# Layer 2 of the edges: one addition ahead of one set of transposes, and a deeper pipeline

## The reference

```
h = x @ W
loops = arange(n); src = [src, loops]; dst = [dst, loops]
deg = number of edges (self loop among them) into each node
out = segment_sum(h[src] / sqrt(deg[src] * deg[dst]), dst) + b
x   = layernorm(x + relu(out))
```

## Time and profile before

| What | us |
|---|---|
| median of 3 runs without a profile | 5666.66 |
| lowest and highest of them | 5656.37, 5669.94 |
| span of the profiled execution | 6076.0 |
| `edges2` in the profiled execution, from its first gather to the start of its last normalising activation | 4285.5 to 4873.0 |

### The profile page before, as it was taken

The page is one execution under the profiler, slowest core; times in us unless marked ns, Lnnn a source line. Parts: engine busy times, 40 slices in busy tenths (PEclk is TensorE's granted clock), DMA queues, the critical chain, the costliest instruction groups (busy, mean ns, idle before and its releaser), DMA issues. The chain is left out here.

```text
span 6076.0 us, 89008 instructions
## 1 busy us (share of the span) xinstructions
PE 4790.3 (79%) x21595; PEld 2959.6 (49%) x21595; DVE 4134.9 (68%) x7958; ACT 3755.8 (62%) x9127; POOL 4234.7 (70%) x4897
## 2 busy tenths in 40 slices
PE   6999999999999879998999899999588844551000
PEld 4555555555555434444444477777466633331000
DVE  5666666666666447777777799999466644557665
ACT  4777777777777534444444488888355555656665
POOL 6777777777777567666776177777666566676776
PEclk9999999999999989999999899999666655655555
DMA  4444444444444425554555499999455477875333
GB/s 109 122 122 124 116 126 120 116 126 119 123 123 116 111 87 174 153 151 148 157 154 147 155 362 363 365 362 343 139 156 158 144 261 243 292 269 171 125 121 98
DMA packets 513957, 1058.78 MB, mean 174 GB/s; under 512 B 123386, under 2 KB 193062, under 8 KB 513732
## 3 DMA queue, kind: packets, MB, share of 16 engines
q1 hardware_dynamic: 408372, 905.58, 44.1%
q0 software_dynamic: 100352, 149.23, 10.7%
q10 hardware_dynamic: 5008, 1.60, 0.1%
HBM read 648.47 MB, written 413.07 MB: 175 GB/s over the span
## 5 line engine op out<-in xcount | busy, mean ns | idle before, releaser
L786 ACT ACTIVATE p_s<-p_ps,cols 128x512 f32<-128x512 f32 x588 | 405.1, 689 | 377.2 <-PE p_ps L728 174.1
L1114 POOL DMA_INDIRECT ring_rows<-t_rows,home_cols x384 | 444.4, 1157 | 232.2 <-issue 91.7
L648 POOL DMA_INDIRECT home<-edge_row_cols,scatter_cols x392 | 428.9, 1094 | 233.6 <-issue 151.4
L147 POOL DMA_INDIRECT u_rows<-t_rows,home_cols x392 | 428.9, 1094 | 220.9 <-issue 116.8
L853 DVE TENSOR_TENSOR p_r<-p_s,p_r 128x512 f32<-128x512 f32 x588 | 402.4, 686 | 257.1 <-ACT p_s L786 188.8
L147 POOL DMA_INDIRECT ring_rows<-t_rows,home_cols x400 | 382.3, 956 | 232.1 <-issue 108.0
L154 POOL DMA_INDIRECT out<-u_res,scatter_cols x392 | 415.1, 1059 | 170.1 <-issue 123.3
L1103 POOL DMA_INDIRECT home_cols<-home,src_cols x380 | 389.3, 1024 | 147.7 <-issue 90.5
L1203 ACT ACTIVATE q_s<-q_ps,cols 128x512 f32<-128x512 f32 x294 | 202.4, 688 | 458.0 <-issue 144.6
L641 POOL DMA_INDIRECT p_xd<-in_x,dst_cols x388 | 408.8, 1054 | 105.2 <-issue 99.0
L641 POOL DMA_INDIRECT p_xs<-in_x,src_cols x388 | 392.7, 1012 | 125.1 <-issue 89.0
(11 more groups left out here) (298 smaller groups left out, 14313.3 us busy)
## 6 DMA issues: line engine op xcount, KB each, us to landing
p_x<-in_x SPq DMA_DIRECT2D x98, 512.0 KB
t_rows<-p_o SPq DMA_DIRECT2D x98, 512.0 KB
hT<-p_r SPq DMA_DIRECT2D x98, 512.0 KB
q_hn<-hT SPq DMA_DIRECT2D x98, 512.0 KB
r_h<-hT SPq DMA_DIRECT2D x98, 512.0 KB
r_x<-t_rows SPq DMA_DIRECT2D x98, 512.0 KB
t_rows<-r_y SPq DMA_DIRECT2D x98, 512.0 KB
t_rows<-r_x SPq DMA_DIRECT2D x98, 512.0 KB
```

The costliest lines, as they stand in the source:

```text
L147: nc.gpsimd.indirect_dma_start(out=rows[:, j, :], out_offset=None, in_=table, in_offset=bass.IndirectOffsetOnAxis(ap=idx[:, j:j + 1], axis ...
L648: nc.gpsimd.indirect_dma_start(out=tab["home"], out_offset=bass.IndirectOffsetOnAxis(ap=s["scat"][:, k:k + 1], axis=0), in_=s["at"][:, k:k ...
L786: nc.scalar.activation(act_out[i][:, :], flat(bank_r), ACT.Silu, bias=col(LS0 + i)).then_inc(r_act[i], 1)
L1114: nc.gpsimd.indirect_dma_start(out=rows[:, e % 4, j, :], out_offset=None, in_=tab["t1"], in_offset=bass.IndirectOffsetOnAxis(ap=s["home"][ ...
```

## The change

- The addition of the own rows moves in front of the transposes: DVE adds `both = rows + own` (both in SBUF, as they were loaded), PE transposes `both` alone, and the scan's result `run` goes straight into the product. The second set of four transposes and its bank `t_ps_t` are gone.
- So that the own row is counted once for each target, `dis` (one over the root of the degree, by which `nodes23` scales the rows it stores) is set to zero for edges that are not the last of their target.
- The four bias matmuls over 9 rows become one over 36 rows and 512 columns; `b2x36` holds the bias parts on a block diagonal, and `sdeg` is loaded as 36 rows of 128 in place of 9 rows of 512.
- The steps are spread: scan two steps behind the addition, product three, sum four, root five, apply six, store nine. All buffers of the stage are four deep. The straight code at the start is 16 steps in place of 8.

```diff
 # setup, nodes01
-  b2x9=sb("b2_x9", [9, H], BF16)
+  b2x36=sb("b2_x36", [9 * G, G, H], BF16)
+  nc.gpsimd.memset(s["b2x36"][:, :, :], 0.0)
-  for k in range(3):
-      sp.dma_start(s["b2x9"][3 * k:3 * k + 3, :], s["b2x3"][:, 0, :])
+  for j in range(G):
+      for k in range(3):
+          sp.dma_start(s["b2x36"][9 * j + 3 * k:9 * j + 3 * k + 3, j, :], s["b2x3"][:, 0, :])
-  nc.vector.reciprocal(s["dis"][:, :], s["sdeg"][:, :])
+  then(nc.vector.reciprocal(s["dis"][:, :], s["sdeg"][:, :]))
+  nc.vector.scalar_tensor_tensor(s["dis"][:, :], s["scat"][:, :], float(SKIP), s["dis"][:, :], ALU.is_lt, ALU.mult)
 # edges2
-  RING, UNROLL, FIRST, LOOP_TO = 8, 8, 8, EB // 8 * 8
+  RING, UNROLL, FIRST, LOOP_TO = 8, 8, 16, EB // 8 * 8
+  TO_SCAN, TO_PRODUCT, TO_GROW, TO_SUM, TO_ROOT, TO_APPLY, TO_STORE = 2, 3, 3, 4, 5, 6, 9
 # POOL
-  after(pool, s_turned, t - RING + 1)
+  after(pool, added, t - RING + 1)
 # PE, step(t)
-  if t.live(EB):
-      transpose4(nc, bank_s[t.of(2)], rows[:, t.of(RING)], s["ident"]).then_inc(s_turned, 1)
-      transpose4(nc, bank_t[t.of(2)], own[:, t.of(8)], s["ident"]).then_inc(o_turned, 1)
-  e = t.back(1)
-      after(pe, summed, e.b - 1)
-      pe.wait_ge(added, e.b + 1)
-      for j in range(G):
-          nc.tensor.matmul(bank_o[e.of(2)][:, j, :], sdeg[:, e.of(8), tile(j)], s["b2x9"][:, :], start=True, stop=False)
-          i = nc.tensor.matmul(bank_o[e.of(2)][:, j, :], both[:, e.of(2), tile(j)], s["w2"][:, :], start=False, stop=True)
+  e = t.back(TO_PRODUCT)
+      pe.wait_ge(scanned, e.b + 1)
+      after(pe, summed, e.b - 3)
+      nc.tensor.matmul(flat(bank_o[e.of(4)]), sdeg[:, e.of(8), :], b2x36 (512 columns), start=True, stop=False)
+      for j in range(G):
+          i = nc.tensor.matmul(bank_o[e.of(4)][:, j, :], run[:, e.of(4), tile(j)], s["w2"][:, :], start=False, stop=j == G - 1)
+  if t.live(EB):
+      pe.wait_ge(added, t.b + 1)
+      after(pe, scanned, t.b - 3)
+      transpose4(nc, bank_s[t.of(4)], both[:, t.of(4)], s["ident"]).then_inc(turned, 1)
 # DVE, step(t): new first instruction, and the lags
+      dve.wait_ge(rows_in[t.of(RING)], landed(RING, t, G))
+      dve.wait_ge(own_in[t.of(8)], landed(8, t))
+      after(dve, turned, t.b - 3)
+      nc.vector.tensor_tensor(both[:, t.of(4)], rows[:, t.of(RING)], own[:, t.of(8)], ALU.add).then_inc(added, 1)
-      nc.vector.tensor_tensor(both[:, t.of(2), :], run[:, t.of(2), :], flat(bank_t[t.of(2)]), ALU.add).then_inc(added, 1)
...
```

More of the change, by code:

```diff
@@ L1697, in ps @@
         def ps(name):
-            return [ctx.enter_context(nc.psum_tensor(f"{name}{i}", [P, G, P], F32)) for i in range(2)]
+            return [ctx.enter_context(nc.psum_tensor(f"{name}{i}", [P, G, P], F32)) for i in range(4)]
         sem = phase_semaphores(nc, ctx, "edges2", sum(to_edges2.values(), []))
-        RING, UNROLL, FIRST, LOOP_TO = 8, 8, 8, EB // 8 * 8
-        rows, own, cont, sdeg = ring["rows"], ring["own"], ring["cont"], sb("t_sdeg", [9, 8, BLK], BF16)
-        run, both = sb("t_run", [P, 2, BLK]), sb("t_both", [P, 2, BLK])
-        degs = sb("t_degs", [P, 2, G])
+        RING, UNROLL, FIRST, LOOP_TO = 8, 8, 16, EB // 8 * 8
+        TO_SCAN, TO_PRODUCT, TO_GROW, TO_SUM, TO_ROOT, TO_APPLY, TO_STORE = 2, 3, 3, 4, 5, 6, 9
+        STEPS = EB + TO_APPLY
+        rows, own, cont, sdeg = ring["rows"], ring["own"], ring["cont"], sb("t_sdeg", [9 * G, 8, P], BF16)
+        both, run = sb("t_both", [P, 4, G, H]), sb("t_run", [P, 4, BLK])
+        degs = sb("t_degs", [P, 4, G])
         od, v, o = sb("t_od", [P, 4, G, H]), sb("t_v", [P, 4, G, H]), sb("t_o", [P, 4, G, H])
@@ L1721, in _ @@
         def _(sp):
-            for t in range(EB + 8):
+            for t in range(EB + TO_STORE):
                 if t < EB:
                     if t >= 7:
-                        after(sp, o_turned, t - 7)
+                        after(sp, added, t - 7)
                         after(sp, grown, t - 7)
@@ L1776, in step @@
                     nc.scalar.activation(sd[:, e.of(4), :], guard[:, e.of(4), :], ACT.Sqrt).then_inc(rooted, 1)
-                if t.live(EB):
-                    act.wait_ge(own_in[t.of(8)], landed(8, t))
-                    act.wait_ge(picked, t.b + 1)
-                    after(act, summed, t.b - 3)
+                e = t.back(TO_GROW)
+                if e.live(EB):
+                    act.wait_ge(own_in[e.of(8)], landed(8, e))
+                    act.wait_ge(picked, e.b + 1)
+                    after(act, summed, e.b - 3)
                     for j in range(G):
-                        i = nc.scalar.activation(od[:, t.of(4), j, :], own[:, t.of(8), j, :], ACT.Copy,
-                                                 scale=degs[:, t.of(2), j:j + 1])
+                        i = nc.scalar.activation(od[:, e.of(4), j, :], own[:, e.of(8), j, :], ACT.Copy,
+                                                 scale=degs[:, e.of(4), j:j + 1])
                     i.then_inc(grown, 1)
-                e = t.back(3)
+                e = t.back(TO_APPLY)
                 if e.live(EB):
@@ L1810, in step @@
                     nc.vector.reciprocal(rs[:, e.of(4), :], sd[:, e.of(4), :]).then_inc(inverted, 1)
-                if t.live(EB):
-                    dve.wait_ge(scanned, t.b + 1)
-                    dve.wait_ge(o_turned, t.b + 1)
-                    after(dve, product, t.b - 1)
-                    nc.vector.tensor_tensor(both[:, t.of(2), :], run[:, t.of(2), :], flat(bank_t[t.of(2)]),
-                                            ALU.add).then_inc(added, 1)
-                e = t.back(2)
+                e = t.back(TO_SCAN)
+                if e.live(EB):
+                    dve.wait_ge(turned, e.b + 1)
+                    dve.wait_ge(cont_in[e.of(8)], landed(8, e))
+                    after(dve, scanned, e.b)
+                    after(dve, product, e.b - 3)
+                    nc.vector.tensor_tensor_scan(run[:, e.of(4), :], cont[:, e.of(8), :], flat(bank_s[e.of(4)]),
+                                                 initial=run[:, e.back(1).of(4), BLK - 1:BLK] if e.past(1) else 0.0,
+                                                 op0=ALU.mult, op1=ALU.add).then_inc(scanned, 1)
+                e = t.back(TO_ROOT)
                 if e.live(EB):
```

58 lines of the change are left out of this document (26 added, 32 removed).

## The result

| | before | changed |
|---|---|---|
| median, us (9 runs each) | 5666.66 | 5679.51 |
| lowest and highest, us | 5656.37, 5670.89 | 5670.21, 5684.39 |
| ratio, with its 95% interval | | 1.0022 (1.0013 to 1.0032) |

The change makes the kernel 12.9 us slower. The forecast was 5596 us, 70 us faster, with a range of 5548 to 5636: wrong in sign.

A forecast was written before the change was run, and what follows sets the result against it. Prediction: a PE-DVE exchange bounds `edges2`; with POOL's pace instead, 461.3 + 18.8 + 10 + 5.6 + 16.8 us end it at 4798.0, a gain of 75.5, scaled to 70: 5596 us, range 5548 to 5636.

The forecast's parts named there:

- What bounds the kernel now: Step on `edges2` before: no engine is full; PE and DVE wait for each other in turn, making 587.5 us.
- the exchange at 5.96 us a block: In `edges2`, DVE's sum waits for PE's product and PE's product for DVE's addition, setting 5.96 us a block.
- the third rival: In `edges2`, unprofiled PE runs at the high clock, POOL already bounds, only the ends move: 5660 us; chance 0.08.
- The runs take 0.933 of the span; I scale.: Whole kernel: unprofiled runs take 0.933 of the profiled span, so the gain of 75.5 us was scaled to 70.
- Order, buffers and pace of the changed stage: Changed `edges2`: the ping-pong goes, POOL sets 5.03 us a block, DVE waits for gathered rows at no cost.
- The worked end of the stage: Changed `edges2`: summed from first gather at 4285.5, its last activation ends at 4798.0, against 4873.5 before.
- The collision: In `edges2`, gathers beginning during L1807, with two SBUF inputs, wait for its end: 18.8 us, bounds 0 and 52.
- The start: Start of `edges2`: PE's instructions arrive late in the straight code, partly covered: 10 us, bounds 0 and 25.
- the rival of the starved straight code: Start of `edges2`: further straight steps deliver PE's matmuls every 1.40 us, 20 us slower, 5686 us; chance 0.04.
- The end: End of `edges2`: 5.6 us for the last gather to land, then 16.8 us of DVE's last steps.
- The exchange isn't there without the profile: Rival on `edges2`: unprofiled, before is already bound by POOL and gains 0 to 15 us, 5660 us; chance 0.08.
- The change doesn't do what it says: Rival on `edges2`: the wait moves to landing gathers, POOL 5.6 us a block, 5635 us; chance counted within the forecast.

The follow-up runs named there:

- e4: The kernel before with one bias matmul of 36 rows and 512 columns in place of four of 9 rows: 6072.55 us, ratio 1.0010.
- e9: The changed kernel with rows and own added by PE in the bank, without the addition on DVE: 6030.04 us, ratio 1.0020.
- e7: The kernel before plus one unread DVE addition a block with both inputs in SBUF: 5683.16 us, ratio 1.0031.
- e8: The kernel before plus one unread DVE addition a block with one input in PSUM: 5671.63 us, ratio 1.0013.
- e15: The changed kernel with rows and own added by PE in the bank, without the addition on DVE, run again: 5668.70 us, ratio 1.0001.
- e16: The changed kernel as it is, run again on the chip of e15: 5678.44 us, ratio 1.0022 to the kernel before.
- e5: The changed kernel as it is, run again on a second chip: 5678.76 us, ratio 1.0021 to the kernel before.
- e6: The kernel before, unchanged, run again for its profile on the chip of e5: 5670.46 us, ratio 1.0007.
- e3: The changed kernel with each lag from the scan on one step shorter: 6137.97 us, ratio 1.0124 to the kernel before.

## Why the prediction was wrong, point by point

**"What bounds the kernel now", the exchange at 5.96 us a block: the step that failed.** The kind that was timed doesn't have the pace of the earlier trace rows. There POOL was the bound (3.7 us of waits in 430). With POOL already full, 75.5 us could not be there to gain. On kind A the change is worth 60 us when POOL has three gathers a block, and nothing before.

The exchange didn't set the 5.96 us on kind B either. The prediction read correctly that PE waits for the addition there. PE's waits from 4300 to 4860 us, in the profile that it read:

```profile
PE t_ps_o L1762 <- issue: 83.4, 45, 6.9
```

The label is "issue", but 29 of these pauses are over 1 us, and every one ends 0.05 to 0.15 us after an addition has ended. In the earlier trace rows the addition ends at 4568.71 and the product starts at 4568.76. What the prediction missed is that POOL pauses in step with this, and not for PE:

```profile
4560.44 1.06 PE L187 MATMUL t_ps_s<-ident,ring_rows 128*128 128x128 f32 x4
...
4561.73 0.95 POOL L147 DMA_INDIRECT ring_rows<-t_rows,home_cols  x1 [0.30 <-issue]
...
4564.86 0.95 POOL L147 DMA_INDIRECT ring_rows<-t_rows,home_cols  x1 [2.18 <-DMA t_rows<-r_y]
```

The gather at 4564.86 is the first of block 53. It needs the transposes of block 45, which ended at 4561.50, before POOL had even stopped at 4562.68. The stage has 44 such pauses, one every eight gathers, and in all of them the needed transposes had ended 3.2 us or more before POOL went on. Together they are 83.9 us over the usual 0.30 us between gathers. That is nearly the whole of the 84.7 us by which the gathers take longer than on kind A (545.6 against 460.9 us between the starts of the first and the last). DVE stands still too, and starts again 0.20 to 0.29 us ahead of POOL, every time. In e4, where PE has less work, the product is long done when both go on:

```profile
4559.73 0.61 PE L1768 MATMUL t_ps_o<-w,t_both 128*128 128x128 f32 x4
...
4563.89 0.69 DVE L1831 SCALAR_TENSOR_TENSOR t_v<-t_ps_o,t_od 128x512 f32<-128x512 f32 x1 [5.01 <-DMA ring_own<-in_edge_attr_T]
4564.19 0.95 POOL L147 DMA_INDIRECT ring_rows<-t_rows,home_cols  x1 [2.15 <-DMA t_rows<-r_y]
```

e9 has such pauses too (45, together 90 us over the usual). So on kind B too the pace is POOL's: eight gathers, 10.06 us, and a pause of 1.9 us more. What stops POOL and DVE there is not shown; no engine's work that they wait for was open in these rows.

A smaller misreading stands beside it. A clock of 0.57, as a mean of 0.5 and 1, is the lower level for 86% of the time, not for half of PE's work. And the third rival's ground, that the low clock comes with PE's idling, is not borne out: e4 idles more (44 us in its 100) and was granted more (0.74).

**"The runs take 0.933 of the span; I scale."** Wrong in form: the 385 us between the spans of before on the two kinds (6053.3 and 5668.4) lie in three stages. `edges1`'s matmuls go from 1171 to 1330 us, `edges2` from 480 to 588, `edges3` from 1080 to 1183 (first gather to last scatter); the rest of the kernel differs by some 15. A span that is 7% over the timed median is a reason to doubt the stage that one wants to gain in, not a factor.

**Order, buffers and pace of the changed stage: right.** POOL without waits, DVE's idle time in front of L1807 and none in front of L1834, 5.14 us a block (472.5 us for 92). PE is at 72 of 100, a little over the 70 that was named. The worked end of the stage was 512.5 us behind its first gather; measured 494.3, as the start and the collision cost 18 us less.

**The collision: mechanism right, size a third to over a half of the forecast.** Predicted 18.8 us. In three executions of the changed kernel gathers averaged 980, 967 and 970 ns against 951: 368 times 29, 16 and 19 ns, 6 to 11 us. A gather that begins while L1807 runs (changed kernel):

```profile
4304.32 0.69 DVE L1807 TENSOR_TENSOR t_both<-ring_rows,ring_own 128x512 f32<-128x512 f32 x1 [0.94 <-DMA ring_rows<-t_rows,home_cols]
4304.64 1.21 POOL L147 DMA_INDIRECT ring_rows<-t_rows,home_cols  x1 [0.30 <-issue]
```

It ends at 4305.85, 0.84 us after the addition, as in the earlier trace rows. e7 against e8 and e15 against e16 show the same cost from both sides. The page of the Trainium skill that the prediction weighed, "SBUF — State Buffer", "Who interferes with whom", has such a `tensor_tensor` leave descriptor generation alone, which it marks as inferred. These four runs (1000 against 954 ns, 952 against 970) decide against it for these gathers, which read their row numbers from `home_cols` in SBUF. By what way the two engines meet isn't shown.

**The start: 10 us predicted, none measured.** The first gathers and transposes of the changed stage:

```profile
4090.89 0.99 POOL L147 DMA_INDIRECT ring_rows<-t_rows,home_cols  x1 [4.26 <-POOLq L37]
4091.04 0.69 DVE L1807 TENSOR_TENSOR t_both<-ring_rows,ring_own 128x512 f32<-128x512 f32 x1
4091.11 2.82 PE L187 MATMUL t_ps_s<-ident,t_both 128*128 128x128 f32 x12 [35.53 <-DVE t_both L1807]
```

Twelve transposes run without a pause. A matmul every 1.40 us, as in the earlier trace rows, was seen in profiles of kind B, and with it the rival of the starved straight code has no ground here.

**The end: 5.6 + 16.8 = 22.4 predicted from the start of the last gather, 22.8 measured; but before needs only 18.8.** (The table counts from that gather's end, 0.96 us later.) The sum came out right by luck: the gather landed in 3.95 us in place of 5.6 (4562.49 to 4566.44 below), and the last steps took 18.8 in place of 16.8. The lags don't make the difference to before, since e15 has them too and needs 16.4 behind the last gather's end. It is the head of DVE's step. The end of the changed kernel, its last gather, last addition and last scan:

```profile
4562.49 0.96 POOL L147 DMA_INDIRECT ring_rows<-t_rows,home_cols  x1 [0.30 <-issue]
...
4566.44 0.69 DVE L1807 TENSOR_TENSOR t_both<-ring_rows,ring_own 128x512 f32<-128x512 f32 x1 [2.24 <-DMA ring_rows<-t_rows,home_cols]
...
4573.93 1.28 DVE L1821 TENSOR_TENSOR_SCAN t_run<-ring_cont,t_run,t_ps_s 128x512 f32<-128x512 bf16 x1
```

And of e15:

```profile
4551.51 0.95 POOL L147 DMA_INDIRECT ring_rows<-t_rows,home_cols  x1 [0.30 <-issue]
...
4557.42 1.28 DVE L1823 TENSOR_TENSOR_SCAN t_run<-ring_cont,t_run,t_ps_s 128x512 f32<-128x512 bf16 x1 [1.04 <-PE t_ps_s L1776]
```

From the last gather's end to the start of the last scan it is 10.5 us in the one and 5.0 in the other. In the changed kernel DVE stands in front of L1807 for the last block's rows with the last three scans (blocks 95 to 97) still to come behind it. The prediction named that wait, put it at nothing in the middle, which holds, and counted it in the end's terms. It had no figure for how short the end of before is on kind A.

**Together.** The profiled stage is 14.6 us longer: 10.6 by the gathers (472.5 against 461.9), 4.0 by the end. Nothing says that those two profiles are of one chip; e5 and e6, which are, differ by 9.6: 5.8 by the gathers, 3.8 by the end. The three timed comparisons say 12.9, 11.3 and 12.5.

**The rivals.** "The exchange isn't there without the profile" (5660, given 0.08) had the bound right, for a wrong reason: it blamed the clock, yet before at kind A runs at 0.70 with POOL full. It left out that without a gain the collision and the end remain, or it would have come to 5667 + 12. The chance for slower was put on starved straight code alone; the plain sum of a change that gains nothing and adds a collision was not among the cases. The upper bound of 5635 in "The change doesn't do what it says" doesn't follow from the terms either: the collision at its worst alone gives 5627, with the start at its worst 5641.

**Open.** What makes a chip one of kind B, and what stops POOL and DVE on it. There, PE's pauses of over 1 us with the label `issue` number 167 in the profile of before, 366 us in all, of which 29 are the waits for the addition told above; counted the same way over the later profile of kind A there is none. Nor was the changed kernel itself run on kind B: its relatives with shorter lags lose 1.1 to 1.4% there, those with the sum on PE nothing, and with three gathers it is behind its twin (504 against 485 us), so nothing there speaks for the predicted gain either. Why shorter lags cost so much on kind B is open too, beyond the waits shown for e3.

No version with all four gathers beats before by more than can be measured. The one that equals it (e15) gets rid of the collision; what would pay, with either pipeline, is fewer or shorter indirect DMAs on POOL, and at three in place of four the changed kernel is worth a further 60 us.

## What to carry to other kernels

Before reading a stage, hold the profile's span against the timed median; where they differ by several per cent, the profile may show another condition, and no stage's share of the difference may be assumed. A printed releaser, "issue" or a DMA, is to be held against the times: what the instruction needs, and when that ended. By this the pauses of PE were waits for the addition, and those of POOL were waits for nothing in its program. Two engines that wait for each other can both be followers of a third. And count the engine with even gaps, such as POOL at 0.95 of every 1.25 us: if its sum is 96% of the stage, no order of the others can gain, and every instruction that lengthens its own work is paid in full.

## What the runs showed of the hardware

- Two kinds of chips, 5666 to 5667 us and 6013 to 6077 us for the same program; the difference lies in three of six stages. In `edges2` of the longer kind, POOL and DVE stand still together every eight gathers, POOL for 2.2 us.
- A DVE addition of 128x512 with both inputs in SBUF lengthened the indirect DMAs beside it, by 49 ns on average (e7 against e6), with an input in PSUM by 3 ns or less (e8 against e6).
- Of two kernels with PE busy 72 and 73 us in the same 100 of `edges2`, the changed one was granted 0.50 (about the lower level, 1.2 of 2.4 GHz) and e15, in which eight plain matmuls against the identity stand for the four transposes (497 matmul records against 257), 0.94:

```profile
4300.00:4400.00 100.00, 73.37 (x497) 62.48 (x496) 65.99 (x162) 60.48 (x184) 75.88 (x80) 0.94 0.66 182
```

PE's longest pause in these 100 us was 3.3 us in the changed kernel and 1.8 in e15. The low clock cost the changed kernel nothing in the middle, where POOL is the pace.
